# Building the token sums from already turned blocks in a linear-attention and routed-bias kernel, with reordered transfers, splits and tail work

## The reference, cut to what matters

```python
xn = layernorm(x)                              # x: (4, 512, 512), read as 2048 tokens x 512
qkv = silu(xn @ w_qkv.T); gate = sigmoid(xn @ w_gate.T)
# lightning attention: 16 heads of 128, blocks of 64, kv carried along the sequence
# per block: o = (q*q_decay) @ kv + ((q @ k.T) * diag_decay) @ v
#            kv = block_decay*kv + (k*k_decay).T @ v
out = norm_w * o * rsqrt(mean(o*o) + eps)
s = (gate * out) @ w_out.T
scores = softmax(xn @ router_w.T + router_bias); topk_w, topk_idx = top_k(scores, 8)
g = silu(xn * sum(topk_w) + sum_k(topk_w * expert_bias[topk_idx]))
return x + s * g
```

## Time and profile before

| what | us |
|---|---|
| median of 3 runs | 1054.85 (1052.76 to 1055.22) |
| the profiled execution, time | 1053.69 |
| its span | 1051.6 |
| PE busy | 1042.0 (99%) |
| DVE busy | 738.0 (70%) |
| POOL busy | 640.2 (61%) |
| ACT busy | 513.1 (49%) |
| DMA, mean busy share of the 16 engines | 45.9% |
| granted TensorE clock | full (1.0) |

### The profile page before, as it was taken

The page is one execution under the profiler, slowest core; times in us unless marked ns, Lnnn a source line. Parts: engine busy times, 40 slices in busy tenths (PEclk is TensorE's granted clock), DMA queues, the critical chain, the costliest instruction groups (busy, mean ns, idle before and its releaser), DMA issues.

```text
span 1051.6 us, 15927 instructions
## 1 busy us (share of the span) xinstructions
PE 1042.0 (99%) x5570; PEld 890.4 (85%) x5570; DVE 738.0 (70%) x1277; ACT 513.1 (49%) x806; POOL 640.2 (61%) x522
## 2 busy tenths in 40 slices
PE   8999999999999999999999999999999999999998
PEld 6988788888888888888888888888888888888887
DVE  6857576676766668777687766767676666776857
ACT  5745355544545345353554545345453543545434
POOL 3467686776867366573656947657474755847511
PEclk9999999999999999999999999999999999999999
DMA  6334727466272533526957354442525335243452
GB/s 237 117 84 120 182 70 203 109 150 176 85 201 65 145 91 91 115 65 162 288 182 182 88 141 131 130 109 64 130 67 133 90 101 101 67 124 90 127 134 81
DMA packets 278110, 132.30 MB, mean 126 GB/s; under 512 B 240400, under 2 KB 240784, under 8 KB 278032
## 3 DMA queue, kind: packets, MB, share of 16 engines
q1 hardware_dynamic: 278032, 131.29, 45.9%
HBM read 89.05 MB, written 42.21 MB: 125 GB/s over the span
## 4 chain that ended last, share of the span: by engine, by line
PE 98%; DVE 1%; DMA 0%; issue 0%; ACT 0%; POOL 0%; SPq 0%; DVEq 0%
PE st_ps L600 18%; PE st_ps L602 18%; PE st_ps L601 18%; PE score_ps L720 5%; PE out_ps L778 5%; PE head_ps L756 5%; PE out_ps L780 5%; PE out_ps L779 5%; PE tk_ps L739 4%; PE head_ps L759 4%; PE st_ps L588 1%; PE st_ps L590 1%; PE st_ps L589 1%; DMA acc<-x_dram 0%; PE v_ps L683 0%; PE v_ps L682 0%
## 5 line engine op out<-in xcount | busy, mean ns | idle before, releaser
L600 PE MATMUL st_ps<-xt_hi,w_hi 128*128 128x512 f32 x826 | 336.6, 408 | 0.0
L602 PE MATMUL st_ps<-xt_hi,w_lo 128*128 128x512 f32 x826 | 323.1, 391 | 0.0
L601 PE MATMUL st_ps<-xt_lo,w_hi 128*128 128x512 f32 x826 | 322.1, 390 | 0.0
L602 PEld LDWEIGHTS st_ps<-xt_hi,w_lo 128*128 128x128 f32 x826 | 155.0, 188 | 34.5
L600 PEld LDWEIGHTS st_ps<-xt_hi,w_hi 128*128 128x128 f32 x826 | 155.6, 188 | 28.8 <-issue 0.3
L601 PEld LDWEIGHTS st_ps<-xt_lo,w_hi 128*128 128x128 f32 x826 | 155.7, 189 | 28.0
L1505 POOL TENSOR_TENSOR w_lo<-land_a,w_hi 128x1024 fp32r<-128x1024 f32 x44 | 107.9, 2452 | 102.2 <-ACT w_hi L1091 102.2
L1485 POOL TENSOR_TENSOR w_lo<-land_a,w_hi 128x768 fp32r<-128x768 f32 x44 | 83.4, 1897 | 117.3 <-ACT w_hi L1086 117.3
L1536 POOL TENSOR_TENSOR acc_sq<-acc_sq,square 128x512 f32<-128x512 f32 x61 | 78.4, 1285 | 37.3 <-ACT square L1181 31.1
L778 PE MATMUL out_ps<-wo_hi,gate_hi 128*128 128x512 f32 x240 | 96.1, 401 | 0.0
L1827 DVE TENSOR_TENSOR acc<-acc,out_ps 128x512 f32<-128x512 f32 x104 | 71.2, 684 | 32.3 <-PE out_ps L780 31.6
(11 more groups left out here) (305 smaller groups left out, 2024.2 us busy)
## 6 DMA issues: line engine op xcount, KB each, us to landing
land_a<-wgrp_dram SPq DMA_DIRECT2D x48, 512.0 KB, 3.6
v_row<-v_squares SPq DMA_DIRECT2D x120, 128.0 KB, 3.2
k_row<-k_squares SPq DMA_DIRECT2D x120, 96.0 KB, 2.9
v_squares<-v_t SPq DMA_DIRECT2D x45, 256.0 KB, 2.7
land_b<-wo_dram SPq DMA_DIRECT2D x16, 512.0 KB, 4.5
land_b<-wgrp_dram SPq DMA_DIRECT2D x14, 512.0 KB, 4.2
k_squares<-state SPq DMA_DIRECT2D x15, 384.0 KB, 2.3
k_squares<-v_t SPq DMA_DIRECT2D x15, 384.0 KB, 4.7
```

The lines of the kernel that those rows point to most:

```text
L600: pe.matmul(ps[:, :], w_h2, x_h2, start=first and k == 0, stop=False, skip_group_check=True)
L601: pe.matmul(ps[:, :], w_h2, x_l2, start=False, stop=False, skip_group_check=True)
L602: end = pe.matmul(ps[:, :], w_l2, x_h2, start=False, stop=last and k == 1, skip_group_check=True)
```

## The change

It takes PE's fills 8 to 15 away, with their `take_fill` on ACT and DVE. Instead ACT writes each of the eight turned banks of fills 0 to 7 back over the rows they came from in `acc` (`keep_fill`, 512 columns each), POOL's `token_sums0` makes the same four differences from these turned rows, ACT's `take_sum` copies each as the high part of its T block (1024 columns), and POOL's new `split_sum` makes the low part. PE's products of step 1 and `scores`, `v_fill(1)`, fills 4 to 7 and the first `head_output` wait on the new semaphores. POOL's opening order becomes: `mask_decay(0)`, `direct_lo(1)`, the sums, one split, `direct_lo(2)`, three splits.

Further: ACT's `sums_hi(1, QK0)` goes behind the key rows and `act_direct(10)`; SP issues `values_back(ss, 1)` ahead of the spills of steps 1 to 4, and the third and fourth spill after the load of the next step's values; ACT's third and fourth `take_block` go behind `out_hi`; POOL's splits of that stage go behind `sums_lo(ss, GATE)`; in step 7 block T2 is renewed ahead of the value weights' load; in `close`, `bias0(2)` goes behind `p6`; and GpSimd adds x to tile 6 of the tail too.

```diff
         squared, gate_h = sem("squared"), sem("gate_h")
+        x_kept, t_high = sem("x_kept"), sem("t_high")
         ln_std, rms_root, seeded = sem("ln_std"), sem("rms_root"), sem("seeded")
...
         summed_v = sem("summed_v")
-        eps_set, zero_set, t_row = sem("eps_set"), sem("zero_set"), sem("t_row")
+        eps_set, zero_set, t_row, t_low = sem("eps_set"), sem("zero_set"), sem("t_row"), sem("t_low")
         block_sum, block_l = sem("block_sum"), sem("block_l")
...
         def rows_of(f):
-            b, half = {B11: (0, 0), B21: (0, 1), B12: (1, 0), B22: (1, 1),
-                       T1: (0, 0), T3: (1, 0), T2: (1, 1), T4: (0, 1)}[f // 2]
+            b, half = {B11: (0, 0), B21: (0, 1), B12: (1, 0), B22: (1, 1)}[f // 2]
             return b, 2 * half + f % 2
         def fill_bank(f):
-            return (out_ps, tk_ps, score_ps, head_ps)[f % 4] if f < 8 else (out_ps, head_ps)[f % 2]
+            return (out_ps, tk_ps, score_ps, head_ps)[f % 4]
+        KEPT = (0, 1, 2, 3, 5, 6, 4, 7)
+        SUMS = (T1, T3, T2, T4)
+        def half_rows(b, half):
+            return acc[:, b, :, half * 256:(half + 1) * 256]
+        def sum_rows(i):
+            return half_rows(*((0, 0), (1, 0), (1, 1), (0, 1))[i]).rearrange("p c (k m) -> p c k m", k=2)
+        def sum_block_at(xt, i):
+            return xt[:, SUMS[i], :, :].rearrange("p k (c m) -> p c k m", c=NCH)
         def direct_bank(j):
...
         tail_out = [st_ps[0], v_ps, out_ps, st_ps[1]]
-        TAIL_POOL = (0, 2, 4)
+        TAIL_POOL = (0, 2, 4, 6)
         def tail_part(n):
...
                     store0(7)
+                values_back(ss, 1)
                 if ss <= 4:
...
                     spill(MADE[(ss - 1) % 2 * 4 + 1], (ss - 1) // 2)
-                values_back(ss, 1)
-                if ss <= 4:
-                    spill(MADE[(ss - 1) % 2 * 4 + 2], (ss - 1) // 2)
-                    spill(MADE[(ss - 1) % 2 * 4 + 3], (ss - 1) // 2)
                 if close:
...
                     load_res(7)
+                if ss == PAIRS - 1:
+                    renew_block(T2, P6)
                 load_group(after, ss + 1, VAL)
+                if ss <= 4:
+                    spill(MADE[(ss - 1) % 2 * 4 + 2], (ss - 1) // 2)
+                    spill(MADE[(ss - 1) % 2 * 4 + 3], (ss - 1) // 2)
                 if ss == PAIRS + 1:
...
                 if ss == PAIRS - 1:
-                    renew_block(T2, P6)
                     renew_block(T1, P5)
...
                 if f >= 4:
-                    pe.wait_ge(xt_l, f - 3 if f < 8 else {8: 5, 9: 8}.get(f, f - 1))
-                if f // 2 in (T1, T3, T2, T4):
-                    pe.wait_ge(t_row, {T1: 1, T3: 2, T2: 3, T4: 4}[f // 2])
+                    pe.wait_ge(x_kept, KEPT.index(f - 4) + 1)
                 for c in range(NCH):
...
             def tokens_there(ss, g, blk):
+                if ss == 1 and g == QK0 and blk in SUMS:
+                    pe.wait_ge(t_low, SUMS.index(blk) + 1)
                 if ss == PAIRS and g == QK0:
...
                 elif f == 1:
-                    pe.wait_ge(xt_l, 6)
+                    pe.wait_ge(xt_l, 8)
+                    pe.wait_ge(x_kept, KEPT.index(5) + 1)
                 else:
...
                 else:
-                    pe.wait_ge(xt_l, 7)
+                    pe.wait_ge(x_kept, KEPT.index(6) + 1)
                 for c in range(NCH):
...
                 if u == 0:
-                    pe.wait_ge(xt_l, 16)
+                    pe.wait_ge(x_kept, 8)
                 elif u == 4 * LAST + 2:
...
                 output_tile(before, 4)
-                if close:
-                    bias0(2)
                 if last:
...
                 p6(ss, QK1)
+                if close:
+                    bias0(2)
                 output_tile(before, 5)
...
             direct_block(3)
-            fill(8)
-            fill(9)
             direct_block(4)
-            fill(10)
-            fill(11)
             turn_and_score(0, 0)
             direct_block(5)
-            fill(12)
-            fill(13)
             v_fill(2)
-            fill(14)
-            fill(15)
             turn_and_score(0, 1)
...
                 act.activation(xt_hi[:, f // 2, f % 2, :], fill_bank(f)[:, :], ACT.Copy).then_inc(xt_h, 1)
+            def keep_fill(f):
+                b, k = rows_of(f)
+                act.wait_ge(xt_l, f + 1)
+                act.activation(acc[:, b, :, k * P:(k + 1) * P], fill_bank(f)[:, :].rearrange("p (c m) -> p c m", c=NCH),
+                               ACT.Copy).then_inc(x_kept, 1)
+            def take_sum(i):
+                act.wait_ge(t_row, i + 1)
+                act.activation(sum_block_at(xt_hi, i), sum_rows(i), ACT.Copy).then_inc(t_high, 1)
             def take_block(blk, k):
...
                 act_c11(ss, QK1)
-                if ss <= 4:
-                    take_block(MADE[(ss - 1) % 2 * 4 + 2], (ss - 1) // 2)
-                    take_block(MADE[(ss - 1) % 2 * 4 + 3], (ss - 1) // 2)
                 if close:
...
                 out_hi(ss, odd)
+                if ss <= 4:
+                    take_block(MADE[(ss - 1) % 2 * 4 + 2], (ss - 1) // 2)
+                    take_block(MADE[(ss - 1) % 2 * 4 + 3], (ss - 1) // 2)
                 if not final:
...
             values_hi()
+            for f in range(4):
+                keep_fill(f)
             root_std(1)
...
                 take_fill(f)
+            keep_fill(5)
             decays(0, 0)
...
             act_direct(3)
-            take_fill(8)
-            take_fill(9)
+            keep_fill(6)
+            keep_fill(4)
+            keep_fill(7)
             for c in range(NCH):
...
             act_direct(4)
-            take_fill(10)
-            take_fill(11)
             take_k_rows(0, 0, 0, 0)
             act_direct(5)
-            take_fill(12)
-            take_fill(13)
+            take_sum(0)
             act.wait_ge(ffn_const_in, 16)
...
             direct_hi(2, 1)
-            take_fill(14)
-            take_fill(15)
+            take_sum(1)
+            take_sum(2)
             take_k_rows(0, 0, 0, 1)
             act_direct(6)
+            take_sum(3)
             take_v(3)
...
             act_direct(9)
-            sums_hi(1, QK0)
             take_k_rows(0, 0, 1, 0)
             act_direct(10)
+            sums_hi(1, QK0)
             take_k_rows(0, 0, 1, 1)
...
             pool.memset(square[:, 0:256], 0.0).then_inc(zero_set, 1)
-            def half_rows(b, half):
-                return acc[:, b, :, half * 256:(half + 1) * 256]
             def token_sums0():
-                pool.wait_ge(ln_row, 8)
-                pool.wait_ge(ln_row_a, 4)
-                pool.wait_ge(xt_turned, 2)
+                pool.wait_ge(x_kept, KEPT.index(4) + 1)
                 pool.tensor_tensor(half_rows(0, 0), half_rows(1, 0), half_rows(0, 0), ALU.subtract).then_inc(t_row, 1)
                 pool.wait_ge(t_row, 1)
-                pool.wait_ge(xt_turned, 6)
+                pool.wait_ge(x_kept, 8)
                 pool.tensor_tensor(half_rows(1, 0), half_rows(1, 1), half_rows(1, 0), ALU.subtract).then_inc(t_row, 1)
                 pool.wait_ge(t_row, 2)
-                pool.wait_ge(xt_turned, 8)
                 pool.tensor_tensor(half_rows(1, 1), half_rows(1, 1), half_rows(0, 0), ALU.subtract).then_inc(t_row, 1)
...
                 pool.tensor_tensor(half_rows(0, 1), half_rows(0, 1), half_rows(1, 1), ALU.subtract).then_inc(t_row, 1)
+            def split_sum(i):
+                pool.wait_ge(t_high, i + 1)
+                pool.tensor_tensor(sum_block_at(xt_lo, i), sum_rows(i), sum_block_at(xt_hi, i).bitcast(F32),
+                                   ALU.subtract).then_inc(t_low, 1)
             def sum_block(blk, k):
...
                 weight_sums(ss, GATE)
+                if close:
+                    finish0(0)
+                    finish0(1)
+                    finish0(2)
+                sums_lo(ss, GATE)
                 if ss in (1, 3):
...
                 if close:
-                    finish0(0)
-                    finish0(1)
-                    finish0(2)
-                sums_lo(ss, GATE)
-                if close:
                     finish0(3)
...
             values_lo()
-            token_sums0()
+            mask_decay(0)
             direct_lo(1, 0)
             direct_lo(1, 1)
-            mask_decay(0)
+            token_sums0()
+            split_sum(0)
             direct_lo(2, 0)
             direct_lo(2, 1)
+            split_sum(1)
+            split_sum(2)
+            split_sum(3)
             out_lo(0)
...
                     else:
-                        dve.wait_ge(xt_turned, 16)
+                        dve.wait_ge(t_low, 4)
                     dve.tensor_copy(dst, out_ps[:, :]).then_inc(acc_set, 1)
...
             dve.wait_ge(ln_stat, LN_DONE[3])
-            take_fill(8)
-            take_fill(9)
             for c in range(NCH):
                 normalise(1, 0, c)
-            take_fill(10)
```

(5 more changed lines are left out.)

## The result

The changed kernel took **1048.75 us** in the median of 5 runs (1048.29 to 1049.78); the kernel before, in 5 runs on the same chip, 1053.54. The ratio is 0.9949, 95% interval [0.9936, 0.9961]: faster by 0.5%. The forecast was 1049.9 in a range of 1048.2 to 1052.0. The profiled execution took 1049.78, the slowest of its five, against 1053.69 of the one before; the spans are 1048.0 and 1051.6, so the traces have 3.6 us to explain where the prediction's sum was 4.9. Another 0.3 us lies outside the span: an execution's time was 2.07 to 2.20 us above its span in every run of the kernel before whose span is on record, and 1.74 to 1.85 in all 68 of the changed kernel and its versions. The prediction had no term for it; as the version with the opening alone (experiment 2) has it too, it came with the opening, and no run shows why.

The account below looks back on a forecast made before the run. PE, at work for 1042.0 of 1051.6 us, was taken as the bound. Terms 3.41 (fills) + 1.4 (values back) + 0.1 (tail) = 4.9 us off the median 1054.85 gave 1049.9 us, range 1048.2 to 1052.0.

Parts of the forecast that it names:

- The fills: Opening: without fills 8 to 15, four pairs between other PE work, PE is 3.41 us earlier from 45 us on.
- `scores(0, 0, 0)`, the tightest: Opening: it needs `keep_fill(6)`, ending by 34.9, and starts at 35.2; margin 0.3 us, priced at nothing, at worst some 0.3.
- POOL's chain: Opening: sums, splits and low parts run from about 35.2 to 68.4 us, with 5.0 us to spare; cost nothing.
- DVE beside POOL: Opening: four DVE operations each wait up to 2.4 us for a POOL instruction; eight `take_fill` fall away; nothing on the path.
- Values back ahead of the spills: Step 1, `kv_products`: `values_back(1, 1)` leaves and issues earlier, so PE's wait goes; 1.4 us gained, bounds 0 to 1.47.
- rival A: The wait at 118 us stays, as the stored values' own landing may set when `values_back` leaves; 1051.3 us, chance 0.13.
- Spills, `take_block`, splits: Steps 1 to 4: `take_block` free at 120.5, `act_c12(QK1)` at 123 to 124, PE wants it at 131.2; nothing.
- Block T2 ahead of the value weights: Step 7: the value weights' transfers come some 1.7 us later, T2 as much earlier; PE waits for neither; nothing.
- `bias0(2)`: Moved behind `p6`: weight load no longer held 0.50 us, but DVE comes to `scale0(2)` at the same time; nothing, bounds ±0.2.
- The tail: DVE ends 0.6 us earlier, but POOL's addition delays tile 6's store; 0.1 gained, bounds 0.6 gained and 0.7 lost.
- rival B: POOL bounds the opening; PE waits at `p6` of step 1 for `sums_lo(1, QK0)` or a T block; 1064.5 us, chance 0.04.
- rival C: The opening gains only in part, with 2 to 5 us given back; 1052 to 1055 us, chance 0.08.

Follow-up runs that it names:

- experiment 2: Kernel before with only the opening changed (fills replaced, later `sums_hi(1, QK0)`), steps 1 to 15 and tail as before: 1049.88 us, ratio 0.9967.
- experiment 1: Changed kernel with `values_back`, the spills, `take_block` and the splits of steps 1 to 4 in their old order: 1049.95 us, ratio 0.9966.
- experiment 3: Changed kernel with block T2 renewed behind the value weights' load in step 7, as before: 1049.02 us, ratio 0.9955.
- experiment 4: Changed kernel with tile 6 of the tail joined on DVE, as before: 1048.31 us, ratio 0.9951.
- experiment 6: Changed kernel with step 7's load of the value weights moved ahead of B21's renewal, right behind `keys_out`: 1048.20 us, ratio 0.9952.
- experiment 9: Experiment 6's kernel with only ACT's third and fourth `take_block` back ahead of `out_hi`: 1062.57 us, ratio 1.0108.
- experiment 11: The changed kernel again, unedited, beside experiment 12 on one chip: 1048.69 us, ratio 0.996.
- experiment 12: Experiment 6's kernel again, unedited, beside experiment 11 on one chip: 1047.31 us, ratio 0.9953.
- experiment 5: Experiment 2's kernel with `values_back(ss, 1)` moved ahead of all spills, `take_block` and splits as before: 1066.54 us, ratio 1.0121.
- experiment 7: Changed kernel with step 7's value weights' load behind two renewed blocks, T2 and T1: 1052.55 us over 11 runs, ratio 0.9987.
- experiment 8: Experiment 6's kernel with third and fourth spills, `take_block` and splits in their old places, `values_back` still ahead: 1065.55 us, ratio 1.0121.
- experiment 10: Experiment 6's kernel with only POOL's splits back ahead of `sums_lo`: 1077.49 us, ratio 1.0228.

## Why the prediction was right, and where not

**The fills** gave 3.42 us for the forecast's 3.41, and all of it arrived: PE's distances between instructions are exact where PE has no idle time. The margins held. `scores(0, 0, 0)`, the tightest, showed no wait; POOL's chain kept the forecast's times to 0.4 us.

**DVE beside POOL** cost nothing on the path. DVE is busy 3.0 us more than before though eight fills of 0.6 went, so the rest of its work takes about 8 us longer; the shared port that the Trainium skill ("SBUF — State Buffer", section "Who interferes with whom") gives as the rule fits, but no experiment here took POOL's work away from beside it.

**Values back ahead of the spills.** I took 1.4 us; the first profile has 1.03, with 0.4 of wait left. The mechanism is shown: without the reordering 1.7 us are back (experiments 1 and 2), and with it the wait was gone in experiments 3, 4, 6, 9, 11 and 12. What remained in the others, 0.4 to 0.9 us, follows the landing of the stored values. In PE's time `values_back(1, 1)` left at 110.8 to 112.2 in the six profiles without a wait, and at 112.9 to 113.6 in the five with one (the changed kernel's first, 112.87, and experiments 5, 7, 8 and 10). My sum let it leave at 111.75. This is what rival A named, and it came about in part.

**"Spills, `take_block`, splits: ... Nothing"** is a step that failed as reasoning, though the moves as I made them cost nothing that repeats. It named no price for the cover gone, and that price is the largest number of the case: with `take_block` left in place the same move makes the kernel 15 us slower, with the splits left in place 30 (experiments 9 and 10). They are not companions of the move, but what it rests on: a transfer that waits on SP until 108.02 was put ahead of spills for which ACT stood at `take_block`. I had the spills leave late enough (by about 117; they were out by 114.86) and `take_block` free at 120.5 (it ran at 115.76 and 118.83), but asked only what stands behind `take_block` in its new place, not what would have stood behind it in the old one. Nor did I look at the weight sums behind the later splits, where ACT waited 2.98 us in the first profile and PE lost 0.30, in one profile of seven.

**Block T2 ahead of the value weights, "PE waits for neither now. Nothing"** is the term of the sum that failed: it cost 1.25 us in the first profile, 1.0 in the second, 0.7 in experiment 1's, nothing in experiment 4's. That PE waits for neither does not say by how much they are early, and I never compared the two. In PE's time the load left 2.0 to 2.8 us later in these four profiles (forecast: about 1.7) and landed 2.6 to 3.9 later, at 517.43 to 518.74 instead of 514.80. Against this the trace of before has 1.7 us from the landing to ACT's use, and 1.0 more until PE feels it: 2.7 in all.

It is not that PE's gain ate the slack. SP's transfers of step 7 wait for PE's own progress and move with it: in PE's time B21's first left at 503.79 in all fourteen profiles, from 6 us ahead of the kernel before to 24 us behind it. What T2 gained by its new place was worth nothing, as PE waited for it in no profile; the block without slack was B22, the last.

**`bias0(2)`**: the load behind it was held 0.50 us before and 0.49 after. Nothing, as forecast. **The tail**: nothing (0.02) for 0.1; experiment 4 confirms that POOL's later store takes what DVE saves.

**The sum.** 3.42 + 1.03 - 0.30 - 1.36 = 2.8 us, and 0.81 by chance at the start, make the 3.6 of the spans; 0.3 outside the span make the 3.9 between the two profiled executions. The forecast of 4.9 came out nearly right for the medians (4.8 in the first set, 3.9 in the second), and that is in part luck: the terms put at nothing took back up to 1.7 us, and the 0.3 outside the span and the earlier first fill, neither of them in the sum, gave up to 1.1. What the four executions without a profile lost in step 8 no trace shows. Rivals B and C did not come about.

## What to carry to other kernels

When a queued transfer is moved ahead, the work it is moved ahead of becomes late by the wait of the moved one, not by its issue time only: follow each of those to the engine that stands for its landing, and price every step that cover rests on, even where the change moves it along. And where nobody waits for a transfer, that is no measure of how early it is: read its landing and its reader's start in the trace of before, and put other transfers ahead of it only within that slack, counting besides their issue that they lengthen its own landing (4.7 us before, 5.3 to 6.4 behind T2). A free stretch of the queue earlier on, as in experiment 6, costs neither.

## What the runs showed of the hardware

- The granted clock of TensorE went to the lower level behind a pause: after 4.81 us without a matmul (experiment 5) it was 0.50 for the next 3.0 us, and 512 columns took 0.43 us from start to start instead of 0.23. The same followed pauses of 3.58 us (experiment 10), 2.62 (experiment 9) and 2.23 (experiment 7), and waits of 2.38 to 2.89 us for the first rows in four profiles (experiments 6, 7, 8, 11). It did not follow such a wait of 2.42 us in the kernel before, of 2.63 in experiment 10, or the pauses under 0.6 us in the changed kernel: the length of the pause alone does not tell it in these rows.
- The four transfers of `values_back(1, 1)` (128 KB each) took 3.0 to 4.1 us to issue with nothing large ahead of them in SP's queue (eleven profiles), and 4.79 to 5.41 with four of 256 KB ahead (three).
- A load of 512 KB took 4.3 us from its issue to where the reader that waited for it ran in one stretch (experiment 10: 124.63 to 128.92), and 5.3 to 6.5 us among the block transfers of step 7 (the changed kernel: 507.43 to 513.88; experiment 4: 506.37 to 511.68). Issued ahead of them it landed in 3.4 to 4.1 us (experiments 6, 8, 9, 10 and 12).
